# Table lookups as one continuous stream over four written-out quads in an attention-FM kernel

## The chip, the cores and the metric

The kernel runs on one core of a Trainium2 chip. The metric is device microseconds of one execution (us), lower is better. A core has TensorE (PE, matmuls; its weight loads are listed as PEld), VectorE (DVE), ScalarE (ACT), GpSimd (POOL) and SyncE (SP, which here only issues DMAs). Each engine works through its own program in order and waits on semaphores.

## The reference, cut to what matters

2048 samples have 26 sparse fields each. A field's id picks a row of 32 floats from that field's table of 12500 rows. All 325 pairs of fields are multiplied, scored by a small two-layer attention, and pooled by a softmax over the pairs.

```python
emb = vmap(lambda tbl, idx: tbl[idx], in_axes=(0, 1), out_axes=1)(embed_tables, sparse)  # 2048 x 26 x 32
bi = emb[:, FIRST, :] * emb[:, SECOND, :]                     # 325 pairs
a = relu(einsum('bpd,dh->bph', bi, att_w_w) + att_w_b)
scores = einsum('bph,ho->bpo', a, att_d_w) + att_d_b
att_out = sum(softmax(scores, axis=1) * bi, axis=1)
out = sigmoid(concatenate([att_out, dense], axis=-1) @ fin_w + fin_b)
```

## The kernel before, in words

The 2048 samples are 16 tiles of 128; four tiles make a **quad**, and the work is a loop over four quads (`QUADS`), a hardware loop (`Fori`) on TensorE, ScalarE and VectorE, and written out on GpSimd.

Within a quad VectorE goes through the fields 0 to 25. For field f it transposes the rows of that field (`turn_field`, L600 and L602) and multiplies them with the transposed rows of all fields before it (`pair_products`, L633), so field f has f pairs. Sixteen pairs are a **group**; there are 21 groups in a quad, in a ring of eight slots (`RING`). TensorE multiplies each group twice (`first_products`, L379, and `final_products`, L389), ScalarE applies the relu (L470), TensorE makes scores of four groups at a time (`score_products`, L403). After 8, 16 and 21 groups sums are transposed back (L418, L426). At the end of a quad there is a tail: the last copies (L661, L663, L666), maximum, exponentials on ScalarE (L527), weighed sums, the division, and the quad's result `pooled` (L697).

The rows themselves come in two ways. Most come by an indirect DMA of GpSimd, one for each tile and field (L332), always one quad ahead: the gather of field f for quad q+1 waits only until field f of quad q is transposed. The others, of the three fields in `LOOK`, are **looked up** on TensorE from a table held in SBUF: partition p holds rows 98p to 98p+97, in 7 chunks of 14 rows. For one tile, seven matmuls (each two passes, hence 14 records in the trace) multiply a one-hot matrix `onehot` by the chunk of the table and add up in the PSUM bank `looked_rows` (L362); VectorE then masks the right one of the 14 rows (`take_looked`, L620) and sums (L623). There is one such bank, so the next tile's first step waits until L620 has read it. A tile is two **steps**, of 4 and of 3 chunks. Before, 10 tiles of a quad are looked up (2 of field 6, 4 of field 14, 4 of field 22), one step beside each of the fields 1 to 20 (`beside`, before the field's last group), and every one of them within the quad that needs it.

The one-hot matrix is made by VectorE (`make_onehots`, L613), one instruction per chunk, from chunk numbers that every partition must see. ScalarE copies the quad's numbers (`look_now`, L508, the first thing in its loop, after its part of the tail of the quad before), and TensorE spreads them over the partitions with one matmul for each tile against the identity (`spread_chunks`, L353), into the PSUM bank that `back_f` uses later. VectorE's own order of work is the order of the code: one-hots for a field come before its transposes, `take_looked` after its pair products.

Of the kernel before, what the change touches and what calls it, by code (L numbers as in the profile page):

```python
# [5 lines left out]
P = 128  # L6
# [11 lines left out]
LOOK = (6, 14, 22)  # L18
LOOK_TILES = (2, 4, 4)
# [3 lines left out]
TABLES_FIRST = 2  # L23
STEPS = (slice(0, 4), slice(4, 7))
STEP_FIRST = 1
SPREAD = (1, 3, 8)
# [3 lines left out]
def layout(n_fields, n_dense):  # L30
    at, cols = 0, {}
    for name, width in (("offset", n_fields), ("w", TILE), ("fin", GROUPS_B * TILE), ("d", 2 * TILE), ("bias_a", 1),
                        ("bias_s", 1), ("dense_w", n_dense), ("fin_b", 1), ("ident", P),
                        ("look_base", 1), ("look_row", CHUNK_ROWS)):
        cols[name] = slice(at, at + width)
        at += width
# [3 lines left out]
def attention_fm(nc, dense, sparse, tables, params, out):  # L40
# [19 lines left out]
    WHOLE = V // PART_ROWS  # L60
    REST = V - WHOLE * PART_ROWS
    assert WHOLE == P - 1 and 0 < REST and CHUNK_ROWS * D <= PAIRS_C * P
    LOOKED = [(n, g) for n in range(LOOKS) for g in range(G - LOOK_TILES[n], G)]
    LOOK_STEPS = len(LOOKED) * len(STEPS)

    def tiles_through_look(n):
        return sum(LOOK_TILES[:n + 1])


    def look_step(f):  # L70

        step = f - STEP_FIRST
        if 0 <= step < LOOK_STEPS:
            return *LOOKED[step // len(STEPS)], step % len(STEPS)

    def looked_tile(f):

        step = look_step(f - 1)
        if step and step[2] == len(STEPS) - 1:
            return step[:2]  # L80

    for n in range(LOOKS):
        assert STEP_FIRST + tiles_through_look(n) * len(STEPS) < LOOK[n]

    def onehots_before(f):


        return [(n, part) for n in range(LOOKS) for part in range(len(STEPS))  # L90
                if f == STEP_FIRST + sum(LOOK_TILES[:n]) * len(STEPS) + part - (0 if n else 1)]

    last = max(f for f in range(F) if onehots_before(f))
    assert SPREAD[-1] < last and last * (last + 1) // 2 < (GROUPS_B + 1) * PAIRS_G

# [53 lines left out]
    with ctx:  # L149
# [12 lines left out]
        wrap = sb("wrap", [P, T, F])  # L162
        moved = sb("moved", [P, T, F])
# [4 lines left out]
        look_table = sb("look_table", [P, LOOKS, CHUNKS, CHUNK_ROWS * D])  # L168
        look_id = sb("look_id", [P, LOOKS, T])
# [3 lines left out]
        look_now = sb("look_now", [P, LOOKS, G])  # L173
# [11 lines left out]
        weighed = sb("weighed", [P, G, PAIRS])  # L185
        neg_max = sb("neg_max", [P, G])
# [29 lines left out]
        chunk_of = back_f[:].rearrange("p c b -> p (c b)")  # L216
# [11 lines left out]
        look_table_zero = sem("look_table_zero")  # L228
        look_id_steps = sem("look_id_steps")
        look_mask_made = sem("look_mask_made")  # L230
        look_now_made = sem("look_now_made")
        chunks_spread = sem("chunks_spread")
# [58 lines left out]
        def _(sp):  # L291
            sp.dma_start(ids[:], sparse.rearrange("(p t) f -> p t f", t=T)).then_inc(ids_in, 16)
            sp.dma_start(feats[:], dense.rearrange("(p t) n -> p t n", t=T)).then_inc(feats_in, 16)
            sp.wait_ge(look_table_zero, 1)

            def load_table(n):

                if n:
                    sp.wait_ge(look_table_in[n - 1], 48)
                whole = tables[LOOK[n], 0:WHOLE * PART_ROWS].rearrange("(p c i) d -> p c (i d)", p=WHOLE, c=CHUNKS)  # L300
                most = WHOLE // 16 * 16
                sp.dma_start(look_table[0:most, n], whole[0:most]).then_inc(look_table_in[n], 16)
                sp.dma_start(look_table[most:WHOLE, n], whole[most:]).then_inc(look_table_in[n], 16)
                rest = tables[LOOK[n]:LOOK[n] + 1, WHOLE * PART_ROWS:].rearrange("f i d -> f (i d)")
                sp.dma_start(look_table[WHOLE:, n].rearrange("p c e -> p (c e)")[:, 0:REST * D], rest
# [459 lines left out]
```

## Time and profile before

| | us |
|---|---|
| median of 3 runs | 505.73 |
| lowest and highest | 505.58, 507.18 |
| profiled execution, its own time | 508.84 |
| profiled execution, span of the trace | 506.6 |
| mean granted TensorE clock in it | 0.951 of full speed |

The span runs from the first to the last instruction; 2.24 us of the profiled execution lie around it. A row of the timeline merges like instructions in a run: its start, how long it lasts, the line and tile, the count, and in brackets the idle time ahead of it with what ended that. "out<-in" names the tile written and the tiles read. A matmul's end is modelled, and a row of them overlaps the next one a little.

### The profile page before, as it was taken

What the parts mean: (1) busy time and instruction counts of PE and PEld (TensorE: products, weight loads), DVE (VectorE), ACT (ScalarE), POOL (GpSimd) and SP (SyncE); (2) the same over time, 40 slices, a digit from 0 to 9 for tenths busy, and PEclk for the clock granted to TensorE, in tenths of its full rate; (3) what the DMA queues carried; (4) which work ended last, traced back from release to release, by engine and by line L of the source; (5) the groups of instructions that cost most, each with busy time, mean ns of one, the idle gap of its engine ahead of it and who ended that gap; (6) DMA issues with size and microseconds to landing.
All of it is one profiled execution on the core that took longest, in us unless ns stands there. A gap on an engine that the chain in (4) does not pass through costs nothing.

```text
span 506.6 us, 6715 instructions
## 1 busy us (share of the span) xinstructions
PE 437.5 (86%) x2248; PEld 172.7 (34%) x2248; DVE 369.5 (73%) x684; ACT 100.8 (20%) x205; POOL 355.6 (70%) x380
## 2 busy tenths in 40 slices
PE   0757897999959898999968899899995899899994
PEld 0423432343225343343324343333223443333321
DVE  8264759677965958966975867987787676877795
ACT  0000110122640001121460011113362001113163
POOL 4777777777777777777777777777777777777400
PEclk9977998999978999999997899999997989999999
DMA  6727232122112232121112222322112222322100
GB/s 175 139 17 140 15 13 14 13 15 13 16 13 13 13 14 13 14 13 14 14 13 13 13 13 13 14 13 14 12 14 12 13 13 13 14 13 13 9 0 1
DMA packets 13242, 11.70 MB, mean 23 GB/s; under 512 B 6448, under 2 KB 12848, under 8 KB 12851
## 3 DMA queue, kind: packets, MB, share of 16 engines
q0 software_dynamic: 12032, 6.18, 21.8%
q1 hardware_dynamic: 912, 5.13, 3.9%
q10 hardware_dynamic: 288, 0.28, 0.2%
q8 instruction: 4, 0.07, 0.1%
q14 instruction: 6, 0.05, 0.0%
HBM read 11.55 MB, written 0.01 MB: 23 GB/s over the span
## 4 chain that ended last, share of the span: by engine, by line
PE 61%; DVE 16%; POOL 9%; issue 8%; ACT 4%; DMA 1%; DVEq 0%; ACTq 0%
PE looked_rows L362 37%; PE first L379 10%; POOL emb L332 9%; PE sums_f L389 8%; DVE ring L633 6%; DVE onehot L613 4%; PE sums_s L403 3%; PE back_f L353 2%; DVE look_masked L620 1%; ACT expd L527 1%; DVE neg_max_early L649 1%; PE back_f L418 1%; PE back_s L426 1%; DMA emb<-tables,rows_first 1%; ACT L508 1%
## 5 line engine op out<-in xcount | busy, mean ns | idle before, releaser
L332 POOL DMA_INDIRECT emb<-tables,rows x326 | 308.0, 945 | 99.3 <-issue 98.1
L362 PE MATMUL looked_rows<-look_table,onehot 128*128 128x448 f32 x560 | 244.2, 584 | 33.2 <-DVE look_masked L620 26.2
L633 DVE TENSOR_TENSOR ring<-emb_t,turned 128x512 f32<-128x512 f32 (+9 forms) x180 | 193.9, 1114 | 3.4
L362 PEld LDWEIGHTS looked_rows<-look_table,onehot 128*128 128x128 f32 x560 | 108.3, 203 | 164.6 <-issue 121.7
L470 ACT ACTIVATE hidden<-first,par 128x512 f32<-128x512 f32 (+1 forms) x84 | 56.5, 677 | 370.3 <-PE first L379 369.9
L379 PE MATMUL first<-ring,par 128*32 128x512 f32 (+1 forms) x672 | 86.7, 592 | 3.1 <-DVE ring L633 2.8
L389 PE MATMUL sums_f<-ring,par 128*32 128x512 f32 (+1 forms) x672 | 88.8, 582 | 0.0
L620 DVE TENSOR_TENSOR look_masked<-looked_rows,look_mask 128x448 f32<-128x448 f32 x40 | 24.9, 622 | 71.5 <-PE looked_rows L362 71.3
L613 DVE TENSOR_SCALAR onehot<-back_f,par 128x512 f32<-128x512 f32 (+1 forms) x84 | 50.0, 654 | 17.2 <-PE looked_rows L362 9.1
L332 POOL DMA_INDIRECT emb<-tables,rows_first x50 | 47.5, 949 | 20.8 <-issue 14.9
L600 DVE STREAM_TRANSPOSE turned<-emb 128x128 f32<-128x128 f32 x100 | 31.9, 319 | 26.6 <-DMA emb<-tables,rows_first 26.4
L389 PEld LDWEIGHTS sums_f<-ring,par 128*32 128x32 f32 x672 | 22.9, 110 | 48.0 <-issue 46.6
L379 PEld LDWEIGHTS first<-ring,par 128*32 128x32 f32 x672 | 14.7, 108 | 59.8 <-issue 41.3
L353 PE MATMUL back_f<-par,look_now 128*128 128x128 f32 x80 | 13.3, 312 | 25.1 <-ACT look_now L508 25.1
L602 DVE STREAM_TRANSPOSE emb_t<-emb 128x128 f32<-128x128 f32 x100 | 27.0, 270 | 0.0
L623 DVE TENSOR_REDUCE emb<-look_masked 128x32 f32<-128x448 f32 x40 | 24.8, 620 | 1.4
L403 PE MATMUL sums_s<-hidden,par 128*32 128x512 f32 (+1 forms) x168 | 25.1, 585 | 0.0
L353 PEld LDWEIGHTS back_f<-par,look_now 128*128 128x128 f32 x80 | 12.1, 217 | 28.8 <-ACT look_now L508 25.8
L403 PEld LDWEIGHTS sums_s<-hidden,par 128*32 128x32 f32 x168 | 5.4, 109 | 16.1 <-issue 9.5
L483 ACT ACTIVATE second_s<-sums_s,par 128x512 f32<-128x512 f32 x12 | 8.2, 688 | 6.0 <-PE sums_s L403 6.0
L426 PE MATMUL back_s<-par,second_s 128*128 128x128 f32 x48 | 7.4, 276 | 1.5 <-ACT second_s L483 1.5
L489 ACT ACTIVATE final<-back_f 128x512 f32<-128x512 f32 (+1 forms) x12 | 6.3, 526 | 10.6 <-PE back_f L418 10.6
(51 smaller groups left out, 94.9 us busy)
## 6 DMA issues: line engine op xcount, KB each, us to landing
emb<-tables,rows POOLq DMA_INDIRECT x326, 3.3
look_table<-tables SPq DMA_DIRECT2D x3, 1372.0 KB
emb<-tables,rows_first POOLq DMA_INDIRECT x50, 3.8
look_table<-tables SPq DMA_DIRECT2D x3, 183.8 KB
par<-params ACTq DMA_DIRECT2D x1, 255.5 KB, 3.1
ids<-sparse SPq DMA_DIRECT2D x1, 208.0 KB, 2.6
feats<-dense SPq DMA_DIRECT2D x1, 104.0 KB, 2.9
look_table<-tables SPq DMA_DIRECT2D x3, 6.8 KB
```

The lines of the kernel that those rows point to most:

```text
L332: pool.indirect_dma_start(emb[:, f, g * D:(g + 1) * D], None, stacked, bass.IndirectOffsetOnAxis(ap=row, axis=0),).then_inc(gathered[f], 16)
L353: mm = nc.tensor.matmul(chunk_of[:, g * P:(g + 1) * P], number, ident, start=True, stop=True)
L362: mm = nc.tensor.matmul(looked_rows, onehot[:, c, g * P:(g + 1) * P], look_table[:, n, c, :], start=c == 0, stop=c == CHUNKS - 1)
L379: mm = nc.tensor.matmul(first[gr % 2][j * TILE:(j + 1) * TILE, 0:n * P], w, ring[:, gr % RING, 0:n, j, :], start=True, stop=True)
L389: mm = nc.tensor.matmul(sums_f[j * TILE:(j + 1) * TILE, 0:pairs_c(gr) * P], row, ring[:, gr % RING, 0:pairs_c(gr), j, :], start=e == 0, st ...
L403: mm = nc.tensor.matmul(sums_s[tile * TILE:(tile + 1) * TILE, cut], d_sel[:, half, :], hidden[:, gr % HIDDEN, cut], start=half == 0, stop= ...
L470: nc.scalar.activation(hidden[:, gr % HIDDEN, cut], first[gr % 2][:, cut], ACT.Relu, bias=par[:, cols["bias_a"]]).then_inc(relu_done, 1)
L600: tr = nc.vector.transpose(turned[:, f % 2, :], emb[:, f, :])
L602: tr = nc.vector.transpose(emb_t[:, f, :], emb[:, f, :])
L613: nc.vector.tensor_scalar(onehot[:, c, tiles], chunk_of[:, tiles], float(-c), par[:, cols["look_base"]], ALU.add, ALU.is_equal).then_inc(o ...
L620: nc.vector.tensor_tensor(look_masked[:], looked_rows.rearrange("p (i d) -> p d i", d=D), mask, ALU.mult).then_inc(look_masked_done, 1)
L633: nc.vector.tensor_tensor(slot[:, at:at + n, :], emb_t[:, i:i + n, :], turned[:, f % 2, :].unsqueeze(1).broadcast_to((P, n, P)), ALU.mult) ...
```

## The change

LOOK becomes fields 3, 11 and 19, with 3, 4 and 4 tiles: 11 tiles of a quad, so 93 gathers where there were 94. The three hardware loops are written out. All 44 tiles form one stream of 88 steps: the first 6 steps (field 3 of quad 0) stand before anything else on TensorE, and each quad has 22 more, one beside each of the fields 1 to 18, 20 and 22 and two in the tail (`END_STEPS`). So the fields 11 and 19 of a quad are looked up in it, and field 3 of the next quad beside fields 17, 18, 20, 22 and in the tail. The last quad has 16 steps, to field 16.

The chunk numbers are no longer spread by TensorE. A new input `look_index` is loaded as 48 rows of 128, VectorE makes chunk numbers of it, SP writes them to a buffer in HBM and reads them back with a broadcast to all 128 partitions, a quad at a time (786 KB each, two buffers). The one-hots are made by one tensor_tensor per step, comparing these numbers with the chunk numbers that a partition holds (a PSUM operand of 7 columns, broadcast). A table is loaded by one DMA over 128 partitions where there were three, and nothing is zeroed first.

```diff
-LOOK = (6, 14, 22)
-LOOK_TILES = (2, 4, 4)
+LOOK = (3, 11, 19)
+LOOK_TILES = (3, 4, 4)
+STEP_FIELDS = (*range(1, 19), 20, 22)
+END_STEPS = 2
...
+    steps = [(q, n, g, part) for q in range(QUADS) for n in range(LOOKS) for g in range(G - LOOK_TILES[n], G)
+             for part in range(len(STEPS))]
+    AHEAD = LOOK_TILES[0] * len(STEPS)
...
+    def steps_beside(q, f):
+        if f == 0:
+            return list(range(AHEAD)) if q == 0 else []
+        at = AHEAD + q * STEPS_Q
+        if f == F:
+            return [i for i in range(at + len(STEP_FIELDS), at + STEPS_Q) if i < len(steps)]
+        return [i for i in [at + STEP_FIELDS.index(f)] if i < len(steps)] if f in STEP_FIELDS else []
...
 @block.sync
             sp.dma_start(ids[:], sparse.rearrange("(p t) f -> p t f", t=T)).then_inc(ids_in, 16)
+            sp.dma_start(index[:], look_index).then_inc(index_in, 16)
...
+            def load_table(n):
+                rows_n = stacked[LOOK[n] * V:LOOK[n] * V + P * PART_ROWS]
+                sp.dma_start(look_table[:, n], rows_n.rearrange("(p c i) d -> p c (i d)", p=P, c=CHUNKS)
+                             ).then_inc(look_table_in[n], 16)
+            def load_chunks(q):
+                if q >= 2:
+                    sp.wait_ge(onehot_made, (q - 1) * (LOOKS * len(STEPS)))
+                sp.dma_start(chunk_of[:, q % 2].rearrange("p n b -> p (n b)"), chunk_numbers[q:q + 1].broadcast_to(
+                    (P, LOOKS * G * P))).then_inc(chunk_of_in[q % 2], 16)
+            load_table(0)
             sp.dma_start(feats[:], dense.rearrange("(p t) n -> p t n", t=T)).then_inc(feats_in, 16)
-            sp.wait_ge(look_table_zero, 1)
...
+            sp.wait_ge(index_chunk_made, 1)
+            sp.dma_start(chunk_numbers.rearrange("q (r p) -> (q r) p", p=P), index_chunk[:]
+                         ).then_inc(chunk_numbers_home, 16)
+            sp.wait_ge(chunk_numbers_home, 16)
+            load_chunks(0)
+            sp.wait_ge(chunk_of_in[0], 16)
+            load_table(1)
+            load_chunks(1)
+            sp.wait_ge(transposed, 6)
+            load_table(2)
+            for q in range(2, QUADS):
+                load_chunks(q)
...
 @block.tensor
-            with pe.Fori(0, QUADS) as q:
-                def spread_chunks(n):
...
+            for q in range(QUADS):
+                def look_up(i):
+                    of, n, g, part = steps[i]
+                    pe.wait_ge(look_table_in[n], 16)
+                    pe.wait_ge(onehot_made, (of * LOOKS + n) * len(STEPS) + part + 1)
+                    if part == 0 and i:
+                        pe.wait_ge(look_masked_done, i // len(STEPS))
...
                 final_products(GROUPS - 2)
+                for i in end_steps[:1]:
+                    look_up(i)
                 score_products(BATCHES - 1)
+                for i in end_steps[1:]:
+                    look_up(i)
                 final_products(GROUPS - 1)
...
 @block.scalar
-                nc.scalar.activation(look_now[:], look_chunk[:, :, bass.ds(q * G, G)], ACT.Copy
-                                     ).then_inc(look_now_made, 1)
...
 @block.vector
-            nc.vector.memset(look_table[P - TILE:].rearrange("p n c e -> p n (c e)")[:, :, REST * D:], 0.0
-                             ).then_inc(look_table_zero, 1)
...
-                    for c in range(STEPS[part].start, STEPS[part].stop):
-                        nc.vector.tensor_scalar(onehot[:, c, tiles], chunk_of[:, tiles], float(-c), par[:, cols["look_base"]],
-                                                ALU.add, ALU.is_equal).then_inc(onehot_made, 1)
+                def make_onehots(of, n, part):
+                    dve.wait_ge(chunk_of_in[of % 2], (of // 2 + 1) * 16)
+                    if of or n:
+                        dve.wait_ge(looked, first_step(of, n) - len(STEPS) + part + 1)
+                    nc.vector.tensor_tensor(onehot[:, chunks, tiles],
+                                            chunk_of[:, of % 2, n, tiles].unsqueeze(1).broadcast_to(shape),
+                                            chunk_here[:, chunks].unsqueeze(2).broadcast_to(shape), ALU.is_equal
+                                            ).then_inc(onehot_made, 1)
...
+                if q == 0:
+                    for i in steps_beside(q, 0):
+                        for of, n, part in onehots_for([i]):
+                            make_onehots(of, n, part)
+                        for tile in tiles_ended([i - 1] if i else []):
+                            take_looked(tile)
...
                 nc.vector.tensor_copy(second_f[:], sums_f[:]).then_inc(second_f_end_done, 1)
+                for tile in tiles_ended(steps_beside(q, F)):
+                    take_looked(tile)
                 dve.wait_ge(back_s_done, (q + 1) * BANKS)
```

## Rows read from the trace of the kernel before

**Rows 1.** The page, busy time of an engine and its share of the span.

```profile
PE 437.5 (86%) x2248; PEld 172.7 (34%) x2248; DVE 369.5 (73%) x684; ACT 100.8 (20%) x205; POOL 355.6 (70%) x380
```

**Rows 2.** Groups by line and shape: busy us, mean ns of one, idle before.

```profile
L332 POOL DMA_INDIRECT emb<-tables,rows x326 | 308.0, 945 | 99.3 <-issue 98.1 <-DVE emb_t L602 1.2
...
L613 DVE TENSOR_SCALAR onehot<-back_f,par 128x512 f32<-128x512 f32 x56 | 38.3, 743 | 9.1 <-PE looked_rows L362 9.1
L600 DVE STREAM_TRANSPOSE turned<-emb 128x128 f32<-128x128 f32 x100 | 31.9, 319 | 26.6 <-DMA emb<-tables,rows_first 26.4
L633 DVE TENSOR_TENSOR ring<-emb_t,turned 128x2048 f32<-128x2048 f32 x12 | 27.4, 2280 | 0.0
...
L633 DVE TENSOR_TENSOR ring<-emb_t,turned 128x1536 f32<-128x1536 f32 x12 | 20.7, 1752 | 0.3
```

**Rows 3.** Timeline of TensorE, its first lookups in quads 1, 2 and 3.

```profile
151.19 8.12 PE L362 MATMUL looked_rows<-look_table,onehot 128*128 128x448 f32 x14 [1.75 <-DVE onehot L613]
159.14 1.05 PE L353 MATMUL back_f<-par,look_now 128*128 128x128 f32 x8
160.17 5.53 PE L362 MATMUL looked_rows<-look_table,onehot 128*128 128x448 f32 x14
...
266.43 1.22 PE L353 MATMUL back_f<-par,look_now 128*128 128x128 f32 x4 [3.95 <-ACT look_now L508]
269.41 7.04 PE L362 MATMUL looked_rows<-look_table,onehot 128*128 128x448 f32 x14 [1.75 <-DVE onehot L613]
...
285.21 7.23 PE L362 MATMUL looked_rows<-look_table,onehot 128*128 128x448 f32 x14 [2.36 <-DVE look_masked L620]
...
388.25 7.35 PE L362 MATMUL looked_rows<-look_table,onehot 128*128 128x448 f32 x14 [1.75 <-DVE onehot L613]
```

**Rows 4.** Timeline of TensorE, quad 2 after that.

```profile
297.33 1.05 PE L353 MATMUL back_f<-par,look_now 128*128 128x128 f32 x8
...
318.76 3.27 PE L362 MATMUL looked_rows<-look_table,onehot 128*128 128x448 f32 x8 [1.44 <-DVE look_masked L620]
...
338.35 3.27 PE L362 MATMUL looked_rows<-look_table,onehot 128*128 128x448 f32 x8
...
370.92 1.07 PE L379 MATMUL first<-ring,par 128*32 128x512 f32 x8
...
376.13 1.50 PE L379 MATMUL first<-ring,par 128*32 128x512 f32 x16 [0.20 <-DVE ring L633]
```

**Rows 5.** Timeline of VectorE, the tail of quad 2.

```profile
379.91 0.69 DVE L661 COPY second_f<-sums_f 128x512 f32<-128x512 f32 x1 [1.72 <-PE sums_f L389]
...
380.93 0.42 DVE L663 COPY score<-back_s 128x256 f32<-128x256 f32 x1 [0.33 <-PE back_s L426]
...
384.38 0.16 DVE L697 TENSOR_TENSOR pooled<-total,inv 128x4 f32 x1
```

**Rows 6.** Timeline of VectorE, the end of quad 3.

```profile
490.86 1.22 DVE L649 TENSOR_REDUCE neg_max_early<-score 128x4 f32<-128x1024 f32 x1 [0.19 <-ACT score L498]
...
492.35 3.62 DVE L633 TENSOR_TENSOR ring<-emb_t,turned 128x512 f32<-128x512 f32 x3
```

**Rows 7.** Timeline of the start, all engines (SPq is SP issuing a DMA).

```profile
5.29 0.34 SPq L302 DMA_DIRECT2D look_table<-tables  x1
...
6.36 1.08 POOL L332 DMA_INDIRECT emb<-tables,rows_first  x1 [5.91 <-DVE rows_first L556]
...
14.77 0.32 SPq L302 DMA_DIRECT2D look_table<-tables  x1
```

**Rows 8.** DMA queue of SP from 8 to 11 us: packets, MB, share of 16 engines.

```profile
q1 hardware_dynamic: 67, 0.84, 106.1%
```

**Rows 9.** The same queue from 13 to 14 us.

```profile
q1 hardware_dynamic: 8, 0.00, 1.2%
```

**Rows 10.** Timeline of TensorE, the first tile that is looked up.

```profile
16.25 7.32 PE L362 MATMUL looked_rows<-look_table,onehot 128*128 128x448 f32 x14 [1.75 <-DVE onehot L613]
```

More of the change, by code:

```diff
@@ L59, in attention_fm @@
     LOOKS = len(LOOK)
[L60 to L64, printed above, removed]
+    assert P * PART_ROWS >= V and P * PART_ROWS - V <= V and LOOK[-1] < F - 1 and CHUNK_ROWS * D <= PAIRS_C * P
+    steps = [(q, n, g, part) for q in range(QUADS) for n in range(LOOKS) for g in range(G - LOOK_TILES[n], G)
+             for part in range(len(STEPS))]
@@ L66, in tiles_through_look @@
+    TILES_Q = sum(LOOK_TILES)
+    STEPS_Q = TILES_Q * len(STEPS)
+    AHEAD = LOOK_TILES[0] * len(STEPS)
+    assert len(STEP_FIELDS) + END_STEPS == STEPS_Q and END_STEPS == len(STEPS)
     def tiles_through_look(n):
         return sum(LOOK_TILES[:n + 1])
[L70 to L94, printed above, removed]
+    def first_step(q, n):
+        return q * STEPS_Q + (tiles_through_look(n) - LOOK_TILES[n]) * len(STEPS)
@@ new lines, in steps_beside, with onehots_for @@
+    def steps_beside(q, f):
[5 more added lines that the diff above has]
+        return [i for i in [at + STEP_FIELDS.index(f)] if i < len(steps)] if f in STEP_FIELDS else []
+    def onehots_for(numbers):
+        return [(steps[i][0], steps[i][1], steps[i][3]) for i in numbers if steps[i][2] == G - LOOK_TILES[steps[i][1]]]
@@ L96, in gathers_of, with tiles_ended @@
+    def tiles_ended(numbers):
+        return [i // len(STEPS) for i in numbers if steps[i][3] == len(STEPS) - 1]
+    for q in range(QUADS):
+        for f in STEP_FIELDS:
+            for i in steps_beside(q, f):
+                of, n = steps[i][:2]
+                assert f + 1 < LOOK[n] if of == q else of == q + 1 and LOOK[n] < f
     def gathers_of(f):
@@ L185, in attention_fm @@
         weighed = sb("weighed", [P, G, PAIRS])
+        wrap, moved = (weighed[:].rearrange("p g e -> p (g e)")[:, i * T * F:(i + 1) * T * F].rearrange(
+            "p (t f) -> p t f", f=F) for i in range(2))
         neg_max = sb("neg_max", [P, G])
@@ L461, in _ @@
             act.wait_ge(par_in, 16)
-            act.wait_ge(look_mask_made, 1)
-            with act.Fori(0, QUADS) as q:
+            for q in range(QUADS):
                 def relu_group(gr):
@@ L644, in _ @@
                             pair_products(f, a, b)
-                    if looked_tile(f):
-                        take_looked(*looked_tile(f))
+                    for tile in tiles_ended(steps_beside(q, f - 1)[-1:] if f else []):
+                        take_looked(tile)
                     if f == EARLY_FIELD:
@@ L661, in _ @@
                 nc.vector.tensor_copy(second_f[:], sums_f[:]).then_inc(second_f_end_done, 1)
+                for tile in tiles_ended(steps_beside(q, F)):
+                    take_looked(tile)
                 dve.wait_ge(back_s_done, (q + 1) * BANKS)
```

132 lines of the change are left out of this document (64 added, 68 removed).

## The prediction

> **What bounds the kernel now.** I read the page first. TensorE is busy for 86% of the span, GpSimd for 70% [rows 1], and neither number decides. For GpSimd the groups by line do: 326 gathers took 308.0 us and 99.3 us stood between them, so one gather costs 1.25 us whatever else runs [rows 2]. From 6.36 us [rows 7] the 376 gathers of four quads end at 476, some 17 us before the last field needs its rows. GpSimd is close behind the others, but does not set the end.
>
> Next I read the timeline of TensorE at the start of each quad, and made a mark of the first lookup: 151.19, 269.41 and 388.25 [rows 3]. So a quad takes 118.2 or 118.8 us, and from the last mark to the end of the span are 118.35. What a quad is made of in quad 2, in three parts: 49.35 us from the mark to the first step of the seventh tile (318.76); 61.15 from there to the copy of VectorE that follows the last group (379.91); 8.34 from that copy to the next mark [rows 3 to 5]. The reader is to see three things there. (a) In the first part TensorE has nothing but lookups, and each time a tile ends it waits until VectorE has emptied the one PSUM bank: 1.03 us (159.14 to 160.17) even if VectorE is free, 2.36 where VectorE was making one-hots, 1.44 at the seventh tile [rows 3, 4]. (b) A tile is a row of 5.53 us, but 8.12, 7.04 and 7.35 after the pause between quads and 7.23 after the wait of 2.36: there the granted clock is at the lower level for part of the row [rows 3]. (c) The third part is a chain through the tail on VectorE, ScalarE's look_now, the spreading matmuls and four one-hot instructions.
>
> **The change, part by part**, against the span of 506.6 us.
>
> *The start.* Before, the first lookup is at 16.25 [rows 10]. Now the first one-hot waits for numbers that go SP, VectorE, HBM, and back. The table's DMA is issued about 3.6 us sooner, behind ids and index; the table before moved at 0.84 MB in 3 us [rows 8], so 1.6 MB and the parameters beside it are through at about 10.4. The write of the numbers stands behind them in the same queue. That small transfers wait there is what the last packets of the old table show: 8 packets of nearly no bytes after 13 us, of a piece issued close behind the big ones [rows 9]. With about 1.5 us for the write, 5.1 for issue, 786 KB at that rate and landing, and 1.8 for the one-hots (a tensor_tensor of 128x1536 took 1752 ns [rows 2]) the first lookup is at 19.0. If nothing queued, it would be 15.5; if the broadcast ran at half that rate and the table as slowly as before (issued 5.29, the next one only at 14.77 [rows 7]), it would be 26. I take 19.0, as the queue is what a row shows. The Trainium skill ("DMA: Bandwidth & Descriptors", section "Queues, rings and completion order") says that descriptors of a ring are consumed in order and that a completion increment lands only after every earlier write of that DMA engine; by this rule it is 19, without it 15.5.
>
> Three tiles in a row follow: 3 x 5.5, plus 1.8 for the clock as in the first tile before (7.32 against 5.53) [rows 3, 10], two changes of tile at 1.0, and 1.6 to the first step beside field 1, since VectorE must make one-hots and take the third tile first: **40.9**. Gathers don't hold this up. Field 10 of quad 0 is there at about 60, and its step comes at 74. VectorE stands in the lookups until about 38 and takes up the fields late, but the rows wait for it, not it for them.
>
> *A quad.* From 118.84:
> - one more tile, of which the two steps lie in the tail, between the last groups: +5.55. Nothing hides it; VectorE's copy comes after the last group, which comes after both steps.
> - waits in the first part. Before: 1.03, 2.43, 0.9 for a spread of 8 records in mid-tile, 1.5; together 5.85 [rows 3, 4]. Now three changes of tile with no group between them at 1.03, and 0.8 where one-hots of field 19 and products of field 9 stand ahead of take_looked: 3.9. So -1.95. The spreads themselves were hidden in the change of tile twice out of three times, and so return little.
> - the clock: 1.5 and 1.7 us were lost in quad 2 [rows 3]. The second goes with the wait of 2.36, the first stays, at the mean of the three marks, 2.0. So -3.2 and +2.0.
> - waits for VectorE's products late in the quad, of 0.2 to 0.35 us: TensorE has more to do there now, -0.6.
> - the third part. The copy at 379.91; then VectorE takes the tile (1.2 us) before the score copy that was at 380.93, and pooled, which was at 384.38 [rows 5], is now at 385.3; a transpose, and one-hots of 128x2048 in 2.28 us [rows 2] instead of look_now, spread and one-hots. The mark is at +8.2: -0.15. The old chain was long, but the new one-hots are twice as large, and take_looked stands in it. It is a swap.
>
> Sum 118.84 + 5.55 - 1.95 - 1.2 - 0.6 - 0.15 = **120.5** for quads 1 and 2. Quad 0 has no pause before its mark: 118.5.
>
> VectorE's one-hots cost less altogether (one of 128x2048 at 2280 ns for four of 743 [rows 2]), but where VectorE is ahead of TensorE this is worth nothing. One gather fewer in each quad frees 5 us of GpSimd, also worth nothing: at my pace GpSimd ends at 470 and its last rows are needed at 491.
>
> *The last quad* has no steps after field 16. Before, the step beside field 17 was at +68.9 (338.35 [rows 4]). Now that point is at 68.9 - 1.95 - 1.2 = 65.8, and the step before it ends at 63.9. TensorE then has only groups, and VectorE becomes the bound: it takes the tile until 65.3, and then makes 172 pairs of fields 18 to 25 at 3.62/25 us (24.9), with transposes of some 0.5 us a field (0.32 each, overlapping [rows 2]) and the early maximum, 1.22 [rows 6]; read off start by start this stretch was 29.4. Products end at 94.7, and from there to the end of the span it was 506.6 - 495.97 = 10.6 [rows 6]. So **105.3**, against 118.35: the two tiles that quads 0 to 2 did for it.
>
> Sum: 40.9 + 118.5 + 241.0 + 105.3 = 505.7, which is 0.9 less than the span of 506.6. The profiled execution took 508.84, 2.24 more than its span, and 3.1 more than the median; the difference carried over to the median gives 505.73 - 0.9 = **504.8**.
>
> *Written out instead of loops.* I put this at nothing. Ahead of dependent small VectorE operations the trace has the same 0.2 us inside the loop and ahead of it, and at the end of a quad all engines wait for the chain above, which would hide a jump. GpSimd's program was already written out and kept its 1.25 us [rows 2]. The Trainium skill ("Runtime: NRT & Kernel Launch", section "Instruction fetch mechanics") holds that a taken branch to a page not loaded stalls the fetch, and prefers unrolled code. By that rule each of three jumps might give something back; by the rows the wait of 3.95 us for ScalarE covered it [rows 3], so both sums are the same unless a stall sat in ScalarE's part.
>
> **The rivals.**
> 1. *The stream starts sooner*: the write and the broadcast pass the table. First lookup at 15.5, end 3.5 us sooner: 501.3. The queue rows speak against it; 0.15.
> 2. *GpSimd's pace*: if the waits in the first part nearly vanish and the clock stays up, gathers bind. Last rows at 6.36 - 1.5 + 372 x 1.25 + 3.4 = 473.3, then 3.9 for the last products and 10.6: 487.8, or 487 as a median. It needs 17 us that I don't find; 0.04.
> 3. *The clock* (slower). TensorE now idles about 7 us between quads with no spreading matmuls in it, and for 1.03 us three times after. If each quad has one more stretch like the 7.23 row, 1.7 us, and the stretch after the pause grows to the longest seen, 2.6, that is 4 x 1.7 + 2 x 0.6 = 8.0: 512.8. It decides from 2.4 us on, that is from two such rows more. For it: the level fell after a wait of 2.36 in two of three quads. Against: after 1.44 the row was 3.27 for 8, full rate [rows 4]. 0.16.
> 4. *The numbers arrive late* (slower): first lookup at 26, 7 us later, all of it on the path: 511.8. The unknown is reading one row of HBM for 128 partitions beside a table; no row shows such a read. 0.15.
>
> **How the numbers follow.** My sum has 0.50; its own range is 500.5 to 508, from the start alone +-2, from the clock and the waits +-1 a quad. Differences of 0.3%, 1.5 us, are about what can be told from no change; that is 504.2 to 507.2. Of the 0.50 I give 0.22 to faster, 0.19 to the same, 0.09 to slower; rivals 1 and 2 are faster (0.19); 3 and 4 go 0.07 to the same and 0.24 to slower. Together faster 0.41, same 0.26, slower 0.33. The range goes to rival 1 and most of the way to 3 and 4: 499 to 511.
>
> **What would show it.** The first lookup at 19; the step beside field 1 of quad 0 at 41; marks of the next quads near 159, 280 and 400; the first part of a quad some 4 us shorter, the second 5 longer; the pause before a mark as long as before, with take_looked in it; the last quad 13 us shorter with TensorE waiting for products. I am wrong if a mark is off by more than 4 us, if VectorE waits for gathers after quad 0, or if one-hots take other than 2.3 us.

## The result, and the profile after

The changed kernel took 503.77 us (median of 20 runs, 502.49 to 507.03), the kernel before 507.19 beside it (median of 20 runs, 505.58 to 509.26). The ratio is 0.9941, with a 95% interval of 0.993 to 0.9953: 3.4 us faster. The prediction was 504.8, in a range of 499 to 511. The profiled execution's span is 502.0 us, against 506.6.

The page's busy times answer to [rows 1]:

```profile
PE 437.5 (87%) x2224; PEld 167.6 (33%) x2224; DVE 364.5 (73%) x637; ACT 96.1 (19%) x198; POOL 351.9 (70%) x376
```

TensorE is busy for exactly as long as before, with four tiles more and no spreading, at a mean granted clock of 0.978 against 0.951. The 4.6 us are idle time that is gone.

The timeline of the start, all engines, answers to [rows 7] and [rows 10] (the number in brackets is the idle time ahead of a row and what ended it):

```profile
5.72 0.33 SPq L325 DMA_DIRECT2D chunk_numbers<-index_chunk  x1
11.62 0.33 SPq L319 DMA_DIRECT2D chunk_of<-chunk_numbers  x1
16.44 0.33 SPq L313 DMA_DIRECT2D look_table<-tables  x1
16.45 3.02 DVE L643 TENSOR_TENSOR onehot<-chunk_of,turned 128x1536 f32<-128x1536 f32 x2 [3.83 <-DMA chunk_of<-chunk_numbers]
...
18.35 7.33 PE L375 MATMUL looked_rows<-look_table,onehot 128*128 128x448 f32 x14 [18.35 <-DVE onehot L643]
...
39.89 5.50 PE L375 MATMUL looked_rows<-look_table,onehot 128*128 128x448 f32 x14 [1.59 <-DVE look_masked L654]
```

SP waits for each piece before it issues the next, so the starts on SP time the chain: write 5.9 us, broadcast 4.8, one-hots 1.9. The step beside field 1 is at 39.89.

TensorE's timeline around the end of quad 1 and in quad 2 answers to [rows 3] and [rows 4]:

```profile
270.46 0.66 PE L426 MATMUL back_f<-par,second_f 128*128 128x128 f32 x4 [0.23 <-DVE second_f L701]
277.72 7.35 PE L375 MATMUL looked_rows<-look_table,onehot 128*128 128x448 f32 x14 [6.61 <-DVE onehot L643]
285.88 5.50 PE L375 MATMUL looked_rows<-look_table,onehot 128*128 128x448 f32 x14 [0.81 <-DVE look_masked L654]
292.19 5.50 PE L375 MATMUL looked_rows<-look_table,onehot 128*128 128x448 f32 x14 [0.81 <-DVE look_masked L654]
...
307.63 5.50 PE L375 MATMUL looked_rows<-look_table,onehot 128*128 128x448 f32 x14 [0.77 <-DVE look_masked L654]
...
323.31 3.25 PE L375 MATMUL looked_rows<-look_table,onehot 128*128 128x448 f32 x8 [0.81 <-DVE look_masked L654]
```

The long row of 7.35 stands after the pause alone. The one that followed the wait of 2.36 in [rows 3] is gone with that wait, and all changes of tile cost the same 0.8.

The chain that ended last holds the marks of the quads, 157.71, 277.72 and 397.45:

```profile
157.71 7.64 PE looked_rows L375 x14
...
277.72 7.37 PE looked_rows L375 x14
...
397.45 7.24 PE looked_rows L375 x14
```

VectorE's timeline of the tail of quad 1, and its copy at the end of quad 2, answer to [rows 5]:

```profile
269.71 0.69 DVE L701 COPY second_f<-sums_f 128x512 f32<-128x512 f32 x1 [7.58 <-PE sums_f L399]
270.32 0.61 DVE L654 TENSOR_TENSOR look_masked<-looked_rows,look_mask 128x448 f32<-128x448 f32 x1
...
274.92 0.16 DVE L739 TENSOR_TENSOR pooled<-total,inv 128x4 f32<-128x4 f32 x1
275.00 0.30 DVE L633 STREAM_TRANSPOSE emb_t<-emb 128x128 f32<-128x128 f32 x1
275.33 2.29 DVE L643 TENSOR_TENSOR onehot<-chunk_of,turned 128x2048 f32<-128x2048 f32 x1
...
389.46 0.69 DVE L701 COPY second_f<-sums_f 128x512 f32<-128x512 f32 x1 [7.58 <-PE sums_f L399]
```

The reader is to see two idle stretches that don't meet. VectorE waits 7.58 us ahead of its copy, while TensorE does the steps of the tail. Then TensorE waits 6.61 us while VectorE goes through the whole tail before it makes the one-hots. Those could have been made in the 7.58.

### The profile page after: what moved, and what is told of

Read it like the earlier page. It is cut to its first block, busy times and chain, and to the rows that moved or that the text cites. A ratio compares the mean times of both kernels' runs of the same rounds, so it can differ in the third digit from the quotient of the medians.

```text
span 502.0 us, 6055 instructions
## 1 busy us (share of the span) xinstructions
PE 437.5 (87%) x2224; PEld 167.6 (33%) x2224; DVE 364.5 (73%) x637; ACT 96.1 (19%) x198; POOL 351.9 (70%) x376
## 4 chain that ended last, share of the span: by engine, by line
PE 75%; DVE 17%; issue 3%; DMA 3%; ACT 2%; DVEq 0%
PE looked_rows L375 48%; PE first L389 12%; PE sums_f L399 10%; DVE ring L667 6%; DVE onehot L643 4%; PE sums_s L413 3%; DVE look_masked L654 3%; DMA chunk_numbers<-index_chunk 1%; ACT expd L538 1%; DVE neg_max_early L689 1%; DMA chunk_of<-chunk_numbers 1%; PE back_f L426 1%; DVE turned L631 1%; DVE emb_t L633 1%; DMA par<-params 1%
## 5 line engine op out<-in xcount | busy, mean ns | idle before, releaser
L375 PE MATMUL looked_rows<-look_table,onehot 128*128 128x448 f32 x616 | 255.5, 562 | 54.1 <-DVE onehot L643 38.1
L375 PEld LDWEIGHTS looked_rows<-look_table,onehot 128*128 128x128 f32 x616 | 115.0, 195 | 195.8 <-issue 195.8
L399 PE MATMUL sums_f<-ring,par 128*32 128x512 f32 (+1 forms) x672 | 86.6, 582 | 0.0
L654 DVE TENSOR_TENSOR look_masked<-looked_rows,look_mask 128x448 f32<-128x448 f32 x44 | 27.3, 621 | 71.4 <-PE looked_rows L375 71.4
L643 DVE TENSOR_TENSOR onehot<-chunk_of,turned 128x1536 f32<-128x1536 f32 (+2 forms) x24 | 44.6, 1861 | 18.2 <-PE looked_rows L375 14.3
L355 POOL DMA_INDIRECT emb<-tables,rows_first x45 | 42.8, 950 | 17.6 <-issue 13.4
L399 PEld LDWEIGHTS sums_f<-ring,par 128*32 128x32 f32 x672 | 21.8, 110 | 48.6 <-issue 47.7
L389 PEld LDWEIGHTS first<-ring,par 128*32 128x32 f32 x672 | 15.5, 108 | 58.0 <-issue 29.5
L657 DVE TENSOR_REDUCE emb<-look_masked 128x32 f32<-128x448 f32 x44 | 27.3, 620 | 1.5
L701 DVE COPY second_f<-sums_f 128x512 f32<-128x512 f32 x4 | 2.8, 692 | 24.4 <-PE sums_f L399 24.4
L496 ACT ACTIVATE second_s<-sums_s,par 128x512 f32<-128x512 f32 x12 | 8.2, 687 | 15.8 <-PE sums_s L413 15.8
L689 DVE TENSOR_REDUCE neg_max_early<-score 128x4 f32<-128x1024 f32 x4 | 4.9, 1220 | 8.0 <-ACT score L511 7.9
L413 PEld LDWEIGHTS sums_s<-hidden,par 128*32 128x32 f32 x168 | 5.3, 109 | 15.8 <-issue 10.3
```

The costliest lines, as they stand in the source:

```text
L355: pool.indirect_dma_start(emb[:, f, g * D:(g + 1) * D], None, stacked, bass.IndirectOffsetOnAxis(ap=row, axis=0),).then_inc(gathered[f], 16)
L375: mm = nc.tensor.matmul(looked_rows, onehot[:, c, g * P:(g + 1) * P], look_table[:, n, c, :], start=c == 0, stop=c == CHUNKS - 1)
L389: mm = nc.tensor.matmul(first[gr % 2][j * TILE:(j + 1) * TILE, 0:n * P], w, ring[:, gr % RING, 0:n, j, :], start=True, stop=True)
L399: mm = nc.tensor.matmul(sums_f[j * TILE:(j + 1) * TILE, 0:pairs_c(gr) * P], row, ring[:, gr % RING, 0:pairs_c(gr), j, :], start=e == 0, st ...
L413: mm = nc.tensor.matmul(sums_s[tile * TILE:(tile + 1) * TILE, cut], d_sel[:, half, :], hidden[:, gr % HIDDEN, cut], start=half == 0, stop= ...
L643: nc.vector.tensor_tensor(onehot[:, chunks, tiles], chunk_of[:, of % 2, n, tiles].unsqueeze(1).broadcast_to(shape), chunk_here[:, chunks]. ...
```

## The experiments

Ratios are to the kernel before, with 95% intervals. e1 to e4 share one chip. e5 to e8 ran on a second and e9 to e12 on a third, where the kernel before took 758 and 762 us: from some 30 us on until the gathers ended, near 620 to 630, TensorE stood in both kernels for up to 36 us at a time with no releaser that the profile shows, which I can't explain. Of those runs I read the start up to the first lookup and the boundaries between quads, the last one above all, and count no ratio of theirs as the kernel's. The ratios of the changed kernel's variants there were 0.9827 (e7), 0.966 (e8), 0.9811 (e10), 0.98 (e11) and 0.9897 (e12), those of the kernel before with ScalarE's loop written out 0.9968 (e5) and 0.993 (e9). The changed kernel itself did not run on these two chips, so none of them sizes an edit.

**e1_before_written_out: is it the loops?** In the kernel before, three lines change:

```diff
-            with pe.Fori(0, QUADS) as q:
+            for q in range(QUADS):
-            with act.Fori(0, QUADS) as q:
+            for q in range(QUADS):
-            with dve.Fori(0, QUADS) as q:
+            for q in range(QUADS):
```

> The kernel before with its three hardware loops written out and nothing else changed. Theory A (the gain comes from TensorE's path: the last quad's two tiles, minus the dearer start and the longer quads): a ratio of 1.000 to the kernel before, within 0.3%; at most 1 us less, from table loads of ScalarE that a loop repeats. Theory B (the gain of 0.6% is that of the straight-line program): 0.994.

503.27 us, ratio 0.993 (0.9911 to 0.9949). The loops alone give as much as the whole change. ScalarE's timeline shows where: before,

```profile
264.43 0.34 ACT L527 ACTIVATE expd<-score,neg_max 128x69 f32<-128x69 f32 x1
264.67 0.19 ACT L527 ACTIVATION_READ_ACCUMULATOR expd<-score,neg_max 128x1 f32 x1
264.87 1.28 ACT L508 ACT_TABLE_LOAD   x1
266.17 0.21 ACT L508 ACTIVATE look_now<-look_chunk 128x12 f32 x1
```

and written out, with TensorE's row behind it:

```profile
263.92 0.19 ACT L527 ACTIVATION_READ_ACCUMULATOR expd<-score,neg_max 128x1 f32 x1
264.01 0.20 ACT L508 ACTIVATE look_now<-look_chunk 128x12 f32<-128x12 f32 x1
...
264.26 0.71 PE L353 MATMUL back_f<-par,look_now 128*128 128x128 f32 x4 [2.53 <-ACT look_now L508]
```

The table load is at the head of each pass of ScalarE's loop, four times before and once at L508 here. It stood in the chain between quads: 3.95 [rows 3] became 2.53 at all three boundaries, which is 4.3 us, where the medians differ by 4.0. The marks are 117.0, 116.5 and 117.3 us apart (the last to the end of the span), against 118.2, 118.8 and 118.35. The last of these has no load in it. Its 1.1 us is what the rows of two tiles make: the third tile of quad 3 took 7.22 before and 5.50 here, the first 7.35 and 8.02. The Trainium skill ("ScalarE activation tables: per-element evaluation and per-set limits", section "Table sets in the compiler and the runtime") says that the compiler's back end places these loads per block; the trace agrees, with one load of 1.28 us per pass of the loop.

**e2_ten_tiles: what do the tiles cost?** In the changed kernel:

```diff
-LOOK_TILES = (3, 4, 4)
+LOOK_TILES = (2, 4, 4)
-STEP_FIELDS = (*range(1, 19), 20, 22)
+STEP_FIELDS = tuple(range(1, 19))
```

> The changed kernel with 10 tiles of a quad instead of 11 (2 of field 3; the steps beside fields 20 and 22 go), so 94 gathers of a quad. Theory A: TensorE loses one tile ahead of the stream (6.3 us) and one in each of the quads 0 to 2 (5.5 each), which would end the span at 479; but GpSimd then ends its 376 gathers at 474.6 and with landing, the last products and the tail the end cannot be before 492. So a span of about 492, ratio 0.975, with VectorE waiting for gathers in the later quads. Theory C (fewer gathers are what the change gained): the span grows by 5 us to 507, ratio 1.004.

494.08 us, ratio 0.9742 (0.9718 to 0.9766), span 492.4. Four tiles less are 22 us of TensorE, of which 9.6 arrive in the span. The chain that ended last shows why:

```profile
by line: POOL emb L355 61.1%; issue 21.0%; PE looked_rows L375 5.7%; DMA emb<-tables,rows 2.8%; DVE ring L667 1.4%; DVE onehot L643 1.3%; PE first L389 0.8%; PE sums_f L399 0.7%; DVE look_masked L654 0.6%; ACT expd L538 0.6%; DMA par<-param
```

Now the gathers lead, end to end at 1.25 us, and VectorE waits for their rows in its transposes:

```profile
L631 DVE STREAM_TRANSPOSE turned<-emb 128x128 f32<-128x128 f32 x100 | 32.1, 321 | 32.0 <-DMA emb<-tables,rows 29.9 <-DMA emb<-tables,rows_first 1.9
```

The last of 376 gathers is issued at 473.84, and the span ends 18.6 us later. The eleventh tile of each quad is there to spare GpSimd four gathers. The four tiles cost TensorE 22 us for 5 us of gathers, and as built that is the dearer way by 9.7 us.

**e3_onehots_early: the pause.** The one-hots of the next quad's first step go ahead of the copy of the last sums:

```diff
-                    for of, n, part in onehots_for(steps_beside(q, f) if f else []):
+                    for of, n, part in onehots_for(steps_beside(q, f) if f > (q > 0) else []):
...
+                for of, n, part in onehots_for(steps_beside(q + 1, 1) if q + 1 < QUADS else []):
+                    make_onehots(of, n, part)
                 dve.wait_ge(finals_done, (q + 1) * GROUPS)
                 dve.wait_ge(back_f_done, q * BANKS + FULL)
                 nc.vector.tensor_copy(second_f[:], sums_f[:]).then_inc(second_f_end_done, 1)
```

> The changed kernel, with the first one-hots of a quad made in the tail of the quad before, while VectorE waits 7.6 us for TensorE's last steps, instead of after the tail. Theory A (the pause between quads is a chain through VectorE, and the 2.3 us one-hots stand in it): the mark of each of the quads 1 to 3 comes 2.3 us sooner, 6.9 us together, span 495, ratio 0.981. Rival (the pause is set by ScalarE or the clock takes the gain back): span between 500 and 502, ratio above 0.990.

495.04 us, ratio 0.9752 (0.972 to 0.9783). TensorE's timeline at the same boundary:

```profile
266.97 0.66 PE L426 MATMUL back_f<-par,second_f 128*128 128x128 f32 x4 [0.23 <-DVE second_f L703]
267.59 3.25 PE L375 MATMUL looked_rows<-look_table,onehot 128*128 128x448 f32 x8
274.42 4.82 PE L375 MATMUL looked_rows<-look_table,onehot 128*128 128x448 f32 x6 [3.58 <-DVE onehot L643]
280.05 7.47 PE L375 MATMUL looked_rows<-look_table,onehot 128*128 128x448 f32 x14 [0.81 <-DVE look_masked L654]
```

The pause of 6.61 is gone. A wait of 3.58 for the second one-hots takes its place, and the rows behind it show the lower clock: 4.82 for 6 records against 2.52, at a granted clock of 0.50, and 7.47. From the last `back_s` products of one quad (L434) to those of the next, or to the end, the profiled execution is shorter than the changed kernel's by 2.0, 0.4 and 3.0 us behind the three boundaries, as these rows come out. Another 1.5 us come before the end of quad 0, from a start that fell early, with which the edit has nothing to do.

**e4_numbers_by_act: does the queue hold up the numbers?** The write and the first broadcast are issued by ScalarE, whose queue has no table in it:

```diff
-            sp.wait_ge(index_chunk_made, 1)
-            sp.dma_start(chunk_numbers.rearrange("q (r p) -> (q r) p", p=P), index_chunk[:]
-                         ).then_inc(chunk_numbers_home, 16)
-            sp.wait_ge(chunk_numbers_home, 16)
-            load_chunks(0)
...
+            act.wait_ge(index_chunk_made, 1)
+            act.dma_start(chunk_numbers.rearrange("q (r p) -> (q r) p", p=P), index_chunk[:]
+                          ).then_inc(chunk_numbers_home, 16)
```

> The changed kernel, with the write of the chunk numbers and the first broadcast issued from ScalarE's DMA queue instead of SP's, where they stand behind the first table. Theory A (they waited in SP's queue): the write takes about 2 us instead of 5.9, the broadcast shares the engines with the table, first lookup at 14 to 15.5 instead of 18.35, span about 499, ratio 0.988. Rival (all transfers share the same engines, so the order of queues gives nothing): first lookup at 18, ratio 0.994.

503.44 us, ratio 0.9926 (0.9898 to 0.9953). The timeline of the start, all engines:

```profile
5.96 0.34 ACTq L471 DMA_DIRECT2D chunk_numbers<-index_chunk  x1
10.86 0.35 ACTq L474 DMA_DIRECT2D chunk_of<-chunk_numbers  x1
...
18.41 7.23 PE L370 MATMUL looked_rows<-look_table,onehot 128*128 128x448 f32 x14 [18.41 <-DVE onehot L644]
```

The write takes 4.9 us in a queue of its own, which lies between the 4.2 and 5.9 of the runs that have it in SP's queue, and the first lookup comes no sooner. Its place in SP's queue is not what makes it slow. Its 64 packets can be told apart here: they moved between 7.75 and 10.25 us, and the last of the table's queue between 10.25 and 10.5.

**e12_numbers_first: then what is?** The write and the first broadcast are issued ahead of the table instead:

```diff
-            load_table(0)
             sp.dma_start(feats[:], dense.rearrange("(p t) n -> p t n", t=T)).then_inc(feats_in, 16)
...
             load_chunks(0)
-            sp.wait_ge(chunk_of_in[0], 16)
+            load_table(0)
+            sp.wait_ge(look_table_in[0], 16)
             load_table(1)
```

> The changed kernel with the write of the chunk numbers and their first broadcast issued ahead of the first table, which is asked for behind them. Theory (the write is slow because it shares the DMA engines with the table's 1.6 MB): it takes about 2 us instead of 4 to 6, the broadcast stays near 4, and the table then sets the first lookup, near 16.5 to 17; the time is that of the change less up to 2 us, a ratio of 0.990 to 0.994. Rival (a write to HBM and its notice take that long by themselves): the write takes 4 us or more as before, the table comes later for it, first lookup at 21 or later and a ratio of 0.998 or more.

The timeline of its start, all engines:

```profile
5.93 0.33 SPq L324 DMA_DIRECT2D chunk_numbers<-index_chunk  x1
7.48 0.33 SPq L319 DMA_DIRECT2D chunk_of<-chunk_numbers  x1
...
12.33 3.01 DVE L643 TENSOR_TENSOR onehot<-chunk_of,turned 128x1536 f32<-128x1536 f32 x2
...
16.75 7.65 PE L375 MATMUL looked_rows<-look_table,onehot 128*128 128x448 f32 x14 [16.75 <-DMA look_table<-tables]
```

With no table under way the write takes 1.55 us, its 64 packets between 6.75 and 7.25, against 4.2 to 5.9 beside one. So it is the table that slows it, from whichever queue. Whether the packets only wait their turn on the engines, or the notice of the write also waits for what the table wrote before it, these runs do not tell. But the table now ends the wait, at 16.75, and e3 and e11 had their first lookups at 16.14 and 15.76 in the old order, with writes of 4.2. With one-hots of this size the start lies between 15.8 and 18.4 whichever way; reordering it is worth nothing that I could show. The ratio on that chip was 0.9897 (0.9869 to 0.9925).

**e5_before_act_out and e9_before_act_again: ScalarE's loop alone.** The edit is the middle pair of lines of e1's.

> The kernel before with ScalarE's loop alone written out; TensorE and VectorE keep theirs. Theory D (what the loops cost the old kernel is the 1.28 us table load that ScalarE repeats at the head of its loop, ahead of look_now, on the chain between quads): pause before look_now's matmuls 2.5 instead of 3.95 us at three of three marks, ratio 0.993, the same as with all loops written out. Rival E (the jump, or the program's fetch, on TensorE and VectorE): ratio 1.000.

> The kernel before with ScalarE's loop over the quads alone written out; the loops of TensorE and VectorE stay. Theory D (what the loops cost is ScalarE's activation table load, 1.28 us, repeated at the head of each pass and standing in the chain between quads): no table load ahead of look_now, its wait 2.5 us instead of 3.95 at all three boundaries, some 1.4 us off each quad, a ratio of about 0.993, as much as with all loops written out. Rival (the jumps of TensorE and VectorE cost it): the ratio is about 1.000 and the marks stay 118.2 to 118.8 us apart.

The timeline of the last boundary of e9, ScalarE and TensorE:

```profile
633.88 0.20 ACT L508 ACTIVATE look_now<-look_chunk 128x12 f32<-128x12 f32 x1
...
634.13 1.05 PE L353 MATMUL back_f<-par,look_now 128*128 128x128 f32 x4 [2.52 <-ACT look_now L508]
```

No table load, and a wait of 2.52; in e5 it is 2.53. The ratios, 0.9968 (0.9942 to 0.9995) and 0.993 (0.9897 to 0.9962), point the same way, but on those chips they size nothing.

**e6_before_pe_dve_out: TensorE's and VectorE's loops alone.** The edit is the other two pairs of e1's.

> The kernel before with TensorE's and VectorE's loops written out and ScalarE's kept. Theory D: ratio 1.000, the pause stays 3.95 us. Rival E: ratio 0.993 to 0.995.

The timeline of its last boundary:

```profile
627.48 1.28 ACT L508 ACT_TABLE_LOAD   x1
628.77 0.21 ACT L508 ACTIVATE look_now<-look_chunk 128x12 f32 x1
...
629.03 0.87 PE L353 MATMUL back_f<-par,look_now 128*128 128x128 f32 x4 [3.96 <-ACT look_now L508]
```

The load is there and the wait is 3.96, as with all three loops [rows 3]. The two jumps cost nothing at this boundary. Together e1, e5, e6 and e9 show that the longer wait between quads is ScalarE's table load, 1.28 us of the 1.4. That nothing else came with the loops is argued and not shown: e6's five runs took 740.1 to 754.3 us, the kernel before beside them 756.2 to 759.8, and the stretch that I can't explain hides what made the difference. What speaks for the load alone is that three waits of 1.42 us make up the 4.0 us of e1.

**e7_after_act_loop: the same load in the changed kernel.** ScalarE's loop is put back:

```diff
-            for q in range(QUADS):
+            with act.Fori(0, QUADS) as q:
```

> The changed kernel with ScalarE's loop put back. Theory D: four table loads again, but the changed kernel's loop begins with the relu of group 0, which waits tens of us for TensorE, so they cost nothing: ratio to the kernel before 0.994, as the changed kernel. So written-out loops would be worth 0.7% in the old kernel and nothing in the new one. Rival E: 1.000.

The timeline of its last boundary:

```profile
626.17 1.28 ACT L483 ACT_TABLE_LOAD   x1
...
629.54 7.02 PE L375 MATMUL looked_rows<-look_table,onehot 128*128 128x448 f32 x14 [6.54 <-DVE onehot L643]
```

The load is back, ScalarE is idle there, and TensorE's pause is the same 6.54. In the changed kernel the load is free.

**e8_warm and e10_warm_again: the clock after the pause.** Seven matmuls that nobody reads, on TensorE at the end of a quad:

```diff
                 finals_back(FULL)
+                if q + 1 < QUADS:
+                    for c in range(7):
+                        nc.tensor.matmul(first[1][:, 0:CHUNK_ROWS * D], ident, look_table[:, 0, c, :],
+                                         start=True, stop=True)
```

> The changed kernel with 7 matmuls of 448 columns into a free PSUM bank in each of the three pauses between quads; their result is not used. They take 5.2 us of the 6.6 us that TensorE idles. If the pause lets the granted clock fall (theory A, its price 1.7 to 2.1 us a quad), the first tile of the quads 1 to 3 takes 5.5 us instead of 7.2 to 7.6, and the span falls by 5 to 6 us to about 496.5, ratio 0.983. Rival: the level falls anyway, or the extra matmuls delay the next tile, ratio 0.994 or more.

> The changed kernel with seven matmuls of 448 columns that nobody reads put into the pause between quads, on TensorE, behind the last products of the quad. Theory (the first tile after a pause costs 7.2 to 7.6 us instead of 5.5 because TensorE stood still): the first tiles of quads 1 to 3 take 5.5 us each, the span is about 496.5 and the ratio to the kernel before about 0.983. Rival (the matmuls delay the copy behind them or what is won is given back as a wait for VectorE): the first tiles are short but the marks stay 120 us apart and the ratio is 0.994, as for the change.

TensorE's timeline at the last boundary of e8:

```profile
622.87 5.43 PE L471 MATMUL first<-look_table,par 128*128 128x448 f32 x14
629.57 5.50 PE L375 MATMUL looked_rows<-look_table,onehot 128*128 128x448 f32 x14 [1.28 <-issue]
```

The first tile behind the pause takes 5.50, in e10 too, and at all three boundaries of both runs, where the changed kernel has 7.64, 7.35 and 7.24. The granted clock was 1.00 over this tile; in the changed kernel it was 0.50 from 277.72 to 279.5, 0.51 to 281.5, and 1.00 after that. From the last `back_s` products of quad 2 (L434) to the end of the span are 110.9 us in both, against 112.7 in the changed kernel, 502.0 - 389.32: 1.8 us for one boundary. On the same two chips it was 112.4 in e7 and 113.6 in e12, with first tiles of 7.02 and 8.20: each time the difference is what the tile is longer than 5.50. For three boundaries that would be some 5.5 us, an estimate; the whole was not measured on an undisturbed chip.

**e11_both_early: all one-hots of the pause.** As e3, for the next quad's first two steps:

```diff
-                    for of, n, part in onehots_for(steps_beside(q, f) if f else []):
+                    for of, n, part in onehots_for(steps_beside(q, f) if f > (2 if q else 0) else []):
...
+                for of, n, part in onehots_for(steps_beside(q + 1, 1) + steps_beside(q + 1, 2) if q + 1 < QUADS else []):
+                    make_onehots(of, n, part)
```

> The changed kernel with the one-hots of the next quad's first two steps both made ahead of the copy of the last sums, four instructions instead of the two of the earlier try. Theory (the pause goes and the wait of 3.6 us for the second one-hots goes with it, until GpSimd's 372 gathers at 1.25 us bind): by TensorE's path the span would be 484.6, by the gathers 4.75 + 372 x 1.25 + 17.65 = 487.4, so about 488, a ratio of 0.965, and TensorE or VectorE wait for gathered rows late in quad 3. Rival (the tail of the quad is held up by the one-hots that now stand in it, so the time only moves): 494 to 495, as with one step's one-hots, a ratio of 0.975.

TensorE's timeline at its last boundary:

```profile
635.59 0.66 PE L426 MATMUL back_f<-par,second_f 128*128 128x128 f32 x4 [1.36 <-DVE second_f L703]
636.21 5.50 PE L375 MATMUL looked_rows<-look_table,onehot 128*128 128x448 f32 x14
644.09 5.50 PE L375 MATMUL looked_rows<-look_table,onehot 128*128 128x448 f32 x14 [2.38 <-DVE look_masked L654]
```

No pause, no low clock at this boundary (1.00), and waits of 2.38 and 1.36 us for VectorE where 0.81 and 0.23 stood, which is the part that the rival named. At the first boundary the wait was 2.06, and the tile behind it took 7.19. From the last `back_s` products to the end of the span are 107.03 us, against 109.65 in e3 and 112.68 in the changed kernel. So the second one-hots are worth another 2.6 us at this boundary, where gathers don't bind. By my estimate the gathers bind from 488 us on; whether the whole comes there was not measured.

## Why the prediction was right

The mechanism held, each term came out a little smaller than I had put it, and one reading beside the sum was wrong. The span was to be 505.7 and is 502.0.

The time was nearer than the sum, and that is luck. The sum promised 0.9 us less than before, and the medians of 20 runs differ by 3.4, the spans by 4.6. But I subtracted the 0.9 from a median of 3 runs, 505.73, which was 1.5 below the 507.19 of 20, and so 504.8 came within 1.0 of 503.77.

| term | predicted | measured |
|---|---|---|
| first lookup | 19.0 | 18.35 |
| from there to the step beside field 1 | 21.9 | 21.54 |
| quad 0 | 118.5 | 117.82 |
| quads 1 and 2 | 120.5 each | 120.01, 119.73 |
| from the last mark to the end | 105.3 | 104.55 |

**A quad in three parts** (quad 2): the first was to shrink from 49.35 to 46.2 and is 45.59 (277.72 to 323.31); the second was to grow to 66.1 and is 66.15; the third was to be 8.2 and is 7.99 (389.46 to 397.45). The term that was mis-sized is the change of tile. I took 1.03 us from the start of the spread to the start of the next tile [rows 3]; without the spread it is 0.77 to 0.81. Two such changes at the start and three in each quad, 14 x 0.22, are 3.1 of the 3.7 us, and the first lookup's 0.65 is the rest, give or take 0.2 us in the third part of a quad.

**The clock.** The price of the pause was put at 2.0 us and is 1.7 to 2.1, and e8 and e10 show that it hangs on TensorE standing still. The low stretch behind the wait of 2.36 went with the wait. So rival 3, one more such stretch in each quad, did not happen. The 1.8 us that I added for the clock in the very first tile came too (7.33), but the profile has the granted clock at 1.00 over that tile, before and after the change, so what makes it long is not shown.

**The start.** The first lookup was right for a reason that holds in part, and with luck. I had the write queue behind the table, and rival 1 had it pass. e4 shows that another queue changes nothing, e12 that an idle set of DMA engines does. In my sum the write ended at 10.4 + 1.5 = 11.9 (11.62 measured), and the broadcast was put at 5.1 (4.8); with 1.8 for the one-hots the terms make 18.8, not the 19.0 that I wrote. Of the two halves of the rule that I weighed, the order in a ring is not what decides, since a ring without the table gave 4.9 us. That a completion lands only after every earlier write of the DMA engine would hold from either queue, and e4 and e12 leave it standing beside plain sharing. The luck is in the run: of the six kernels that start exactly alike (the changed one, e3, e7, e8, e10 and e11) the first lookup came between 15.76 and 18.35, so e3 and e11 lie close to rival 1's 15.5, with writes that still took 4.2. Rival 4's broadcast at half rate didn't come.

**The step that failed is "Written out instead of loops. I put this at nothing."** I looked for the cost of a jump and found none, and at the boundary between quads there is none (e6). But the row of 3.95 [rows 3] held a table load that the loop repeats, 1.28 us in each of three pauses, and with the loops written out the kernel before is as fast as the changed one (e1: 0.993; the change: 0.9941; the intervals overlap). My total did not suffer, because the new third part was priced from rows that have no `look_now` in them, so the load fell out unseen. But I called that part "a swap", and it was one only because the old side carried 1.4 us that three edited lines would have removed. Against the written-out kernel before, the stream, the eleventh tile and the numbers by DMA gain nothing together that can be told. By the marks of e1 and of the changed kernel the first lookup of quad 1 comes 7.9 us later, quads 1 and 2 take 3.0 and 3.2 us more, and the last quad takes 12.7 less: 1.4 us more in the span.

**Rival 2, GpSimd's pace,** had the smallest chance, and on this kernel it needed 17 us that weren't there. In e2, with four tiles less and four gathers more, it is what binds.

**A version that beats both.** e2 at 494.08 and e3 at 495.04 are both measured on the undisturbed chip, 2.6% and 2.5% faster than the kernel before. Against the changed one, measured apart from them, that is 1.9% and 1.7% less, of which in e3 some part can be a start that fell early.

## What to carry to other kernels

Look in the trace of every loop for instructions that nobody wrote, at the head of a pass: a table load there costs nothing where its engine waits anyway, and its full time where its engine is the link between two passes. When two engines wait for each other one after the other, as VectorE's 7.58 and TensorE's 6.61 here, move the work that needs nothing new into the first wait; the kernel with three lines so edited took 1.7% less than the changed one (e3). Before work is moved from one engine to spare another, price both: a lookup of 5.5 us for a gather of 1.25 paid nothing here, where the gathers did not bind.

## What the runs showed of the hardware that I had not expected

- An activation table load of 1.28 us is repeated at the head of each pass of ScalarE's hardware loop (four in the kernel before, at L508; four in e7), and is there once when the quads are written out.
- A write of 24 KB to HBM took 1.55 us with no large load under way, and 4.2 to 5.9 us beside a load of 1.6 MB, from SP's queue (4.2 to 5.9) and from ScalarE's (4.9) alike. The broadcast behind it took 3.7 to 5.6. For the two, the same start varied by 2.6 us between runs.
- After a pause of 6.5 to 6.6 us TensorE's first 14 matmuls of 448 columns took 7.0 to 8.4 us (7.02 in e7, 8.38 in e2) instead of 5.5, at a granted clock of 0.50 at first; matmuls that filled the pause brought back all of it. After a wait of 2.53 in e1 one row of three was long (7.20) and two ran at the full rate, and after 2.36 in the kernel before two of three were long (7.23 and 7.22); what decides there stays open.
- On two of the three chips of the experiments both kernels took half as long again, with TensorE standing still while gathers ran and no cause in the profile. That stays open too.
